# Forgetting attention: the key gates added inside VectorE's maxima, the output product on GpSimd, the roundings with a per-partition factor

## The reference

```
k, v = silu(conv4(x @ Wk)), silu(conv4(x @ Wv));  q = x @ Wq      # conv4: causal, 4 taps, per channel
q, k = rms_norm(q) * qnw, rms_norm(k) * knw                        # over the 64 channels of a head
c    = cumsum(log_sigmoid(x @ Wf + bf), over time)                 # one row per head
s    = q @ k.T / sqrt(64) + c[query] - c[key]                      # keys after the query are masked
o    = softmax(s) @ v
out  = (rms_norm(o) * onw * silu-like gate(x @ Wg)) @ Wo
```

## Time and profile before

| | |
|---|---|
| median of 3 runs | 2142.07 us (2141.72 to 2145.16) |
| the profiled execution | 2145.37 us, span 2143.5 us |
| the units of the stage in the trace | about 780 to 1735 us, the even part about 860 to 1640 us |
| busy over the whole span | TensorE 85%, VectorE 79%, ScalarE 66%, GpSimd 48% |

### The profile page before, as it was taken

The page is one execution under the profiler, slowest core; times in us unless marked ns, Lnnn a source line. Parts: engine busy times, 40 slices in busy tenths (PEclk is TensorE's granted clock), DMA queues, the critical chain, the costliest instruction groups (busy, mean ns, idle before and its releaser), DMA issues. The chain is left out here.

```text
span 2143.5 us, 36549 instructions
## 1 busy us (share of the span) xinstructions
PE 1823.9 (85%) x12003; PEld 880.1 (41%) x12003; DVE 1687.6 (79%) x2282; ACT 1409.8 (66%) x2322; POOL 1033.2 (48%) x1121
## 2 busy tenths in 40 slices
PE   5558886686978758999999999999999867789997
PEld 2113332553665413555555555555554423222222
DVE  5979997695349778888888888888887636698884
ACT  3547774574347646877777777777776524689994
POOL 0167774173106515666666776666666521431112
PEclk9869999798999989999999999999999978899999
DMA  3000000000000011112121121111111100422210
GB/s 97 0 15 0 0 0 0 1 0 1 0 0 1 1 58 52 53 63 60 51 62 62 63 62 58 62 56 59 63 63 62 36 16 20 99 79 56 59 47 40
DMA packets 71432, 84.49 MB, mean 39 GB/s; under 512 B 20544, under 2 KB 44032, under 8 KB 71168
## 3 DMA queue, kind: packets, MB, share of 16 engines
q1 hardware_dynamic: 69536, 81.69, 12.6%
q10 hardware_dynamic: 1728, 0.67, 0.1%
HBM read 71.95 MB, written 9.57 MB: 38 GB/s over the span
## 5 line engine op out<-in xcount | busy, mean ns | idle before, releaser
L1771 DVE SCALAR_TENSOR_TENSOR fu_kv<-fu_ps_kv,fa_vec,fu_kv 128x511 f32<-128x511 f32 (+2 forms) x384 | 285.7, 745 | 56.1 <-ACT fu_kv L1643 51.1
L1854 POOL TENSOR_TENSOR fu_ds<-fu_p 128x768 f32<-128x768 f32 x64 | 115.8, 1809 | 194.3 <-PE fu_ps_ss L1542 191.8
L2209 ACT ACTIVATE rt_p<-rt_ps_s 128x1024 f32<-128x1024 f32 x192 | 185.6, 1028 | 25.1 <-PE rt_ps_s L2140 25.1
L1502 PE MATMUL fu_ps_s<-fu_qn,fu_kn 64*128 64x512 f32 (+3 forms) x1024 | 190.0, 468 | 2.5 <-DVE fu_sg L1732 1.8
L625 POOL TENSOR_TENSOR scan_hC<-scan_h,scan_c 128x1024 f32<-128x1024 f32 x64 | 150.8, 2356 | 72.0 <-DVE scan_h L601 72.0
L1643 ACT ACTIVATE fu_kv<-fu_ps_kv,fa_vec 128x512 f32<-128x512 f32 x128 | 88.3, 690 | 111.0 <-PE fu_ps_kv L1551 66.6
L1532 PE MATMUL fu_ps_n<-fu_p,fu_vt 128*64 128x512 f32 (+3 forms) x1024 | 151.9, 439 | 0.0
L524 PE MATMUL scan_ps_y<-scan_hC,w_ident 128*128 128x512 f32 x256 | 125.7, 614 | 26.4 <-POOL scan_hC L625 14.9
L601 DVE TENSOR_TENSOR_SCAN scan_h<-scan_dA,scan_ps_b 128x1024 f32<-128x1024 f32 x64 | 146.4, 2287 | 2.2
L2105 POOL TENSOR_SCALAR rt_d<-rt_d 128x1024 f32<-128x1024 f32 x32 | 34.9, 1091 | 184.1 <-DVE rt_d L2230 178.4
L1870 POOL TENSOR_TENSOR fu_kn<-fu_ks,fu_rb 128x512 f32<-128x512 f32 x64 | 81.4, 1272 | 75.2 <-DMA fu_rb<-rms_rows 75.0
(11 more groups left out here) (384 smaller groups left out, 5291.4 us busy)
## 6 DMA issues: line engine op xcount, KB each, us to landing
fu_rb<-rms_rows SPq DMA_DIRECT2D x256, 128.0 KB, 2.9
fu_ro<-rms_rows SPq DMA_DIRECT2D x128, 128.0 KB, 3.0
ra_stackq<-rope_parts SPq DMA_DIRECT2D x168, 32.0 KB
ra_stackk<-rope_parts SPq DMA_DIRECT2D x168, 32.0 KB
w_X<-in_xT SPq DMA_DIRECT2D x4, 512.0 KB, 6.6
fa_wp<-in_wp SPq DMA_DIRECT2D x8, 256.0 KB
fa_cr<-ncum_rows SPq DMA_DIRECT2D x128, 3.0 KB
rope_parts<-ra_hi SPq DMA_DIRECT2D x16, 128.0 KB, 3.1
```

The source lines that it names most:

```text
L1502: pe.matmul(sps[:, h, at:at + T - t * P], k[head(h), t * P:(t + 1) * P], q[head(h), t * P:T], start=(at == 0), stop=False)
L1771: dve.scalar_tensor_tensor(acc, kvps[:, at, 0:T - j], vec[:, a % GA, w:w + 1], acc, ALU.mult, ALU.add).then_inc(done, 1)
L1854: pool.tensor_tensor(DS[:, :, :], P0[p % 2][:, :, P:T], P13[:, :, 0:3 * P], ALU.add).then_inc(s.d1, 1)
L2209: act.activation(p[:, :, :], sps[unit(g, t, i) % RING][:, :, :], ACT.Exp, scale=DH_B ** -0.5).then_inc(s.exp, 1)
```

## The change

Four edits. (1) The key gates are no longer added by TensorE: the 8 matmuls per unit with `w_pick` go. Instead `cum` is stored to DRAM in fp32 (`ncum`), two rows per unit are loaded with broadcast to 128 partitions (`fu_nb`, 512 KB, one DMA, behind the 4 loads of `fu_rb`), and VectorE adds them while it takes the maximum, by `tensor_tensor_reduce`, one instruction per head and block. (2) The output product `fu_og` moves from VectorE to GpSimd; its per-channel weight is folded into `fa_wo` once. (3) The roundings, which can no longer take a negated maximum, multiply by a per-partition -1 (`w.neg`) in `scalar_tensor_tensor`. (4) The loads of `fu_nb` wait until the maxima of the unit that held the buffer before are done.

```diff
 # forget_gates, SP
+                sp.wait_ge(s.cum, 1)
+                sp.dma_start(ncum_dram, cum[:, :]).then_inc(held.kept, 16)
 # forget_units, SP, behind the four loads of RB
+                        row = HEADS_A * n + 2 * g
+                        sp.wait_ge(s.red, seen(u - 1, 2 * NT))
+                        sp.dma_start(NB[u % 2][:, :, :], ncum_dram[row:row + 2, :].rearrange("(o h) t -> o h t", o=1).broadcast_to([P, 2, T])).then_inc(nbs[u % 2], 16)
 # TensorE
-                    for t, at in blocks:
-                        for h in range(2):
-                            pe.matmul(mps[:, h, at:at + (t + 1) * P], w.pick[head(h), :], cr[head(h), 0:(t + 1) * P], start=False, stop=False)
-                        pe.wait_ge(crs[m % 3], 32 * (m // 3 + 1))
 # VectorE
+                def greatest(u, t, at):
+
+                    cols = (t + 1) * P
+                    for h in range(2):
+                        sums = mps[:, h, at:at + cols]
+                        dve.tensor_tensor_reduce(sums, sums, NB[u % 2][:, h, 0:cols], 1.0, LOWEST, ALU.add, ALU.max, top[:, t, h:h + 1]).then_inc(s.red, 1)
-                        dve.tensor_reduce(nm[:, 1, :], mps[:, :, 0:2 * P], AX_X, ALU.max, negate=True).then_inc(s.red, 1)
+                        greatest(b, 1, 0)
-                        dve.tensor_copy(MHL[:, :, :, 3], nm[:, :, :]).then_inc(s.hi, 1)
+                        dve.scalar_tensor_tensor(MHL[:, :, :, 3], top[:, :, :], w.neg[:, 0:1], MHL[:, :, :, 0], ALU.mult, ALU.mult).then_inc(s.hi, 1)
-                        dve.tensor_tensor(MHL[:, :, :, 4], nm[:, :, :], MHL[:, :, :, 3], ALU.subtract).then_inc(s.ml, 1)
+                        dve.scalar_tensor_tensor(MHL[:, :, :, 4], top[:, :, :], w.neg[:, 0:1], MHL[:, :, :, 3], ALU.mult, ALU.subtract).then_inc(s.ml, 1)
-                    if real(o):
-                        output(o)
 # GpSimd, behind the gated numerator and ahead of the root's iterations
+                    if real(o):
+                        pool.wait_ge(s.gated, o + 1)
+                        pool.wait_ge(ros[o % 2], 32 * (o // 2 + 1))
+                        pool.wait_ge(s.wo, o // 2)
+                        pool.tensor_tensor(OG[o % 2][:, :], NUM[o % NR][:, :], RO[o % 2][:, :], ALU.mult).then_inc(s.og, 1)
```

More of the change, by code:

```diff
@@ L1249, in forgetting_attention_stages, with forget_gates @@
 def forgetting_attention_stages(nc, w, X, XN):
+    ncum_dram = nc.dram_tensor("ncum", (P, T), F32, kind="Internal").ap()
     ncum_rows = nc.dram_tensor("ncum_rows", (P, KF, T), BF16, kind="Internal").ap()
     with Stage(nc, "fa") as outer:
-        loaded, stored = outer.sems("loaded stored")
+        loaded, stored, kept = outer.sems("loaded stored kept")
         held = named(
             wp=outer.sb("wp", [P, GA, 4, P]), wo=outer.sb("wo", [P, GA, P]), vec=outer.sb("vec", [P, GA, 3 + 2 * TAPS]), nc=outer.sb("nc", [P, KF, T], BF16), cr=[outer.sb(f"cr{k}", [P, T], BF16) for k in range(3)], mhl=outer.sb("mhl", [P, NT, 2, DH_A], BF16),
-            loaded=loaded, stored=stored,
+            loaded=loaded, stored=stored, kept=kept,
         )
-        forget_gates(nc, w, XN, ncum_rows, held)
-        forget_units(nc, w, X, XN, ncum_rows, held)
-def forget_gates(nc, w, XN, ncum_rows, held):
+        forget_gates(nc, w, XN, ncum_dram, ncum_rows, held)
+        forget_units(nc, w, X, XN, ncum_dram, ncum_rows, held)
+def forget_gates(nc, w, XN, ncum_dram, ncum_rows, held):
     with Stage(nc, "fg") as st:
@@ L1328, in _, with forget_units @@
                 dve.tensor_copy(NC[:, 2, :], r2[:, :]).then_inc(s.lo, 1)
-def forget_units(nc, w, X, XN, ncum_rows, held):
+def forget_units(nc, w, X, XN, ncum_dram, ncum_rows, held):
     U = B * GA
@@ L1337, in forget_units @@
     KR, VR, NR = 7, 3, 6
+    LOWEST = -3.0e38
     THIRDS = ((0, slice(0, P)), (1, slice(P, 320)), (3, slice(320, T)))
@@ L1388, in forget_units @@
         RR = st.sb("rr", [P, T], BF16)
-        nm = st.sb("nm", [P, NT, 2])
+        top = st.sb("top", [P, NT, 2])
+        NB = [st.sb(f"nb{k}", [P, 2, T]) for k in range(2)]
         SG = st.sb("sg", [P, T])
@@ L1450, in _ @@
                 sp.wait_ge(held.stored, 16)
+                sp.wait_ge(held.kept, 16)
                 for i in range(-AHEAD, U + OUT + 2):
@@ L1568, in _ @@
                         g = o % GA
-                        pe.wait_ge(s.red, seen(b + 1, 4))
+                        pe.wait_ge(s.red, seen(b + 1, 2 * NT))
+                        pe.wait_ge(s.set, 5)
+                        pe.wait_ge(s.x, o // 2)
                         pe.wait_ge(s.og, o + 1)
@@ L1761, in _ @@
                 dve.wait_ge(held.loaded, 16 * (GA + 2))
+                dve.wait_ge(held.kept, 16)
                 for i in range(-AHEAD, U + 1):
@@ L1830, in _ @@
                 add(last - 3)
-                output(last - 2)
                 begin(U + 1)
                 gate(last + 1)
-                output(last - 1)
                 add(last - 1)
-                output(last)
-                output(last + 1)
                 add(last + 1)
@@ L1845, in _ @@
                 pool.tensor_scalar(qw[:, :], qw[:, :], 0.5 * DH_A ** -0.5, None, ALU.mult).then_inc(s.set, 1)
+                pool.memset(SG[:, :], 0.0).then_inc(s.set, 1)
                 pool.tensor_scalar(ow[:, :], vec[:, :, 2], 0.25, None, ALU.mult).then_inc(s.set, 1)
-                pool.memset(SG[:, :], 0.0).then_inc(s.set, 1)
-                for i in range(-AHEAD, U + OUT + 1):
-                    d, p, c, u = i + AHEAD - 1, i - 1, i - OUT, i + 2
+                pool.wait_ge(s.set, 4)
+                pool.tensor_tensor(wo[:, :, :], wo[:, :, :], ow[:, :].rearrange("p (g o) -> p g o", o=1).broadcast_to([P, GA, P]), ALU.mult).then_inc(s.set, 1)
+                for i in range(-AHEAD, U + OUT + 2):
+                    d, p, c, o, u = i + AHEAD - 1, i - 1, i - OUT, i - OUT - 1, i + 2
                     if real(p):
@@ L1874, in _ @@
                         pool.tensor_tensor(NUM[c % NR][:, :], NUM[c % NR][:, :], SG[:, :], ALU.mult).then_inc(s.gated, 1)
-                    q, o = windows(i - 2) if i % WIN == 0 else (None, None)
-                    if q is not None or o is not None:
-                        j, r = (i - 2) // WIN + 3, slice(0, rows_of(q, o).stop)
+                    if real(o):
[3 more added lines that the diff above has]
+                        pool.tensor_tensor(OG[o % 2][:, :], NUM[o % NR][:, :], RO[o % 2][:, :], ALU.mult).then_inc(s.og, 1)
+                    q, v = windows(i - 2) if i % WIN == 0 else (None, None)
+                    if q is not None or v is not None:
+                        j, r = (i - 2) // WIN + 3, slice(0, rows_of(q, v).stop)
                         if j < ENDING:
@@ L2302, in hybrid_kernel @@
         for name in EARLY + LATER:
-            tile(name, BF16 if name in ("pick", "eye2", "mask2", "past2", "identb") else F32)
+            tile(name, BF16 if name in ("eye2", "mask2", "past2", "identb") else F32)
         for name, shape in (("u0", [P, P]), ("vo0", [P, P]), ("bias1", [P, 1]), ("gate", [P, FF]), ("up", [P, FF]), ("down", [P, KF, P]),
```

30 lines of the change are left out of this document (12 added, 18 removed).

## The result

The changed kernel takes 2165.96 us in the median of 4 runs (2157.10 to 2169.12), beside 2143.61 for the kernel before in the same runs: a ratio of 1.0104 [1.0085, 1.0122], so 22 us slower. The forecast was 2131, faster. The profiled execution took 2162.96 us, with a span of 2160.9.

What follows compares the result with a forecast made beforehand. TensorE was taken as the bound, VectorE hardly behind. Each pair gains 0.44 us less 0.1 for the roundings, 0.34 times 32 = 11 us: 2134.4 for the profiled execution, so 2131 against 2142.07; 8-in-10 range 2113 to 2163.

Steps and rivals of the forecast that it cites:

- What bounds the kernel, and the pair: Even part of the stage: TensorE bounds, VectorE hardly behind; a pair of steps takes 27.4 us instead of 27.78.
- TensorE's saving, and the price of the new instructions: Per unit: TensorE saves 0.55 us without `w_pick`; VectorE's maxima cost 0.15 us fixed per half, +0.87 in all.
- Rival 1: VectorE's maxima cost the upper bound, 0.31 us per half; 21 us slower, 2163; chance 0.22.
- The roundings, "a loose end" of 0.1 us per pair: Short step: roundings slip ahead of GpSimd's third sum, 0.4 us earlier, or are held, 0.25 later; 0.1 us per pair lost.
- I see no reason why they should be freer.: VectorE's new roundings read two SBUF tiles, so GpSimd instructions hold them as they held the cast, 0.69 us.
- Which may push `fu_ro` by 3 us; then GpSimd waits inside the 5.63.: Long step: the `fu_nb` load ahead may delay `fu_ro` 3 us, within GpSimd's 5.63 us of idle time.
- Rival 5: Long step: `fu_og` on GpSimd holds VectorE's query by 0.6 us, 19 us in all; 2150; chance 0.08.
- 0.44 gained: The pair of steps closes 0.44 us early, before 0.1 us is taken off for the roundings.
- Rival 3: Short step: the new rounding is free of GpSimd, 0.20 us instead of 0.69; 27 us gained, 2115; chance 0.10.
- Rival 4: Edits cancel: fixed part near 0.2 us, rounding held in most steps (0.3 per pair); 2.6 us gained, 2139.5; chance 0.15.
- The DMA wait caps TensorE's lead: VectorE's bit operation, ahead of block 1's maximum, waits for `fu_var`'s DMA and is only 0.11 us early; TensorE's 0.4 is lost.
- The 14 us ahead of the roundings' term: Whole stage: 32 pairs, each 0.44 us shorter, gain 14 us before the roundings' 0.1 us per pair is subtracted.

Runs made afterwards that it cites:

- experiment 4: Changed kernel with roundings reading the maxima from PSUM (negating reduction, cast, subtraction: three instructions for two); 2127.98 us, 0.9916 of the kernel before.
- experiment 2: Kernel before with only `fu_og` moved from VectorE to GpSimd, old maxima and roundings; 2148.15 us, 1.0017 of the kernel before.
- experiment 1: Changed kernel with `fu_og` back on VectorE ahead of the query; 2159.44 us, 1.0076 of the kernel before.
- experiment 3: Changed kernel with the load of `fu_nb` issued behind the store of the roots and the loads of `fu_ro`; 2177.45 us, 1.0160 of the kernel before.
- experiment 9: Changed kernel with `fu_og` on GpSimd replaced by two memsets of its tile, which read nothing; 2175.78 us, 1.0159 of the kernel before.
- experiment 5: Changed kernel with roundings from PSUM and the `fu_nb` load behind the roots' store and `fu_ro` loads; 2116.37 us, 0.9873 of the kernel before.
- experiment 10: Experiment 5 with the root's bit operation moved behind the roundings of the next step; 2106.24 us, 0.9832 of the kernel before.
- experiment 7: Kernel before with only the roundings changed, to read the maxima from PSUM; 2134.49 us, 0.9961 of the kernel before.
- experiment 8: Kernel before with `fu_og` on GpSimd and roundings reading the maxima from PSUM; 2128.39 us, 0.9932 of the kernel before.
- experiment 6: Changed kernel with roundings from PSUM and `fu_og` back on VectorE; 2141.00 us, 1.0001 of the kernel before.

## Why the prediction was wrong

- **What bounds the kernel, and the pair.** Right for one half of the pairs: 13 took 27.35 to 27.71 us, where 27.4 was forecast. They are not free of holds; their roundings cost as much as in the pairs of 27.78 before (1.7 us, where those took 1.7 to 2.1). The stage got slower by the other half.
- **TensorE's saving, and the price of the new instructions.** The mechanism was right and the term too dear: about 0.1 us fixed per half, 0.15 taken. Rival 1, for which the pitch of 512 columns had to be above 0.75 us, is false, with a pitch of 0.60 and 0.65. That its 2163 lies near the measured 2166 is chance.
- **The roundings, "a loose end" of 0.1 us per pair.** This is the step that failed. The working put one hold against one place of the old schedule, the start of the short step, and let GpSimd move by 0.55 us with TensorE. At that place the roundings rose from 0.93 to 1.19 us. The larger part came at the start of the long step, which the working left out (1.04 us before, 1.56 after, from 0.5 to 3.5): there the sums do not wait for TensorE but follow the root, and the prediction itself had the root end 1.3 us later. Measured over all: 0.35 us per unit more than before, 0.7 per pair, where 0.1 was taken. A small part is the new form itself, which takes 0.26 and 0.25 us when free, against 0.18 and 0.20 of the old one. In experiment 4, where nothing holds them, the result changes its sign, by 38 us. The row that should have warned was already there: a cast of 8 columns at 0.69 us beside a remainder at 0.20 says that the chain behind it costs whatever GpSimd happens to do.
- **"I see no reason why they should be freer."** Right, but the second rounding became less free, which was not asked. Where the first is held by one partial sum, the second and the next sum start within 0.02 us of each other. The old remainder started within 0.005 us of the sum in 45 units and was held in none; in 6 it came 0.006 us or more behind, and was held. In experiment 2, with the old form, it was 52 free and none held. The new form came 0.006 to 0.016 us behind the sum in all 31 such units of the changed kernel, and in 43 to 51 each of experiments 1, 3 and 9, and was held every time. No run changes the form of the roundings alone, so what this costs in time stays open.
- **"Which may push `fu_ro` by 3 us; then GpSimd waits inside the 5.63."** The wait was there, but GpSimd had also come later, and `fu_og` ran beside the query. Idle ahead of `fu_og` is now 90 us in the 740 read, and ahead of the first sum 32, where 161 stood. Rival 5 had just this mechanism, with a chance of 0.08, since it asked for a landing within half a microsecond of one place. It needs no such luck: an instruction of 1.27 us and one of 0.74 overlap over a width of 2 us, 42 of 56 did, and 33 of them were held. It took 0.32 us per unit on VectorE, 0.64 per pair, where rival 5 had 0.6. But it seems to have cost little time here: the short pairs have the longer queries, and experiments 1, 3 and 9, with free queries, took 2159 to 2177 us.
- **The two together** add 1.3 us per pair on VectorE, against 0.44 gained. The pair became 0.6 longer and not 0.9. The roundings' 0.7 less the 0.44 gives 0.3 of the 0.6; what makes up the rest no run separates.
- **Rivals.** Rival 3 (a free rounding) described what experiment 4 then built, 2128 against its 2115, the query being held. Rival 4's reason, a held rounding, was right, and its 0.3 us per pair less than half of what came.
- **The DMA wait caps TensorE's lead.** Right: in experiment 5 it is 0.64 us, and moving it off the chain (experiment 10) gives 10 us.
- **The 14 us ahead of the roundings' term.** Not confirmed as it stands. With free roundings on both sides the edits as they were made gain 7 us (experiment 4 against 7; 9, each against its own kernel before), with the query held. With the gate load also behind the store, which is no part of the change, they gain 18 (5 against 7): the move of `fu_og` is 6 of them (8 against 7) and the gates in the maxima 12 (5 against 8), in this order. The other way round they don't add up so (experiment 6).

The Trainium skill (page "SBUF — State Buffer", section "SBUF: two separate sides") says that VectorE and GpSimd share a pair of ports, locked for a whole instruction: a VectorE instruction with two SBUF inputs fully blocks against a GpSimd one that reads SBUF. The runs agree: the query takes 0.74 us beside fills and up to 1.83 behind a product that started first, and the roundings with one input in PSUM take 0.19. The prediction named this rule and drew from it only that the new form was no better; what it did not ask is how often each such instruction meets one of GpSimd's.

Open is why the new form of the rounding comes a hundredth of a microsecond later than the old one, and why experiment 6 stands 7 us above experiment 7.

## What to carry to other kernels

Before work moves to GpSimd, list VectorE's instructions with two SBUF inputs on the critical chain (and copies within SBUF, as the cast here), the smallest first, at every place of the period: each can cost a whole GpSimd instruction, and a shift of either engine moves the collision and does not remove it. Remove it by the form (one operand in PSUM), and only then judge a change of order, whose sign may turn: the later gate load lost 11 us before that and gained 9 to 12 after. A period that varies from pair to pair, as 27.5 and 29.7 here, can be a sign of such meetings; sort the pairs by the time of the suspected instructions to see which of them pays. A steady period is no proof of the opposite: in experiment 3 nearly every pair had the same hold.

## What the runs showed of the hardware

- A maximum with an accumulator write shows as two instructions in the trace, but costs only about 0.1 us beyond its columns, since the write (0.14 us) overlaps the next one.
- The hold works both ways: in experiment 4 `fu_og` took 1.56 us where it takes 1.27, started 0.32 us behind a query. Between 0.04 and 0.33 us behind a query it took 1.56 to 1.84 us in all five cases, and the query 0.74 or 0.75.

```profile
1238.27 0.74 DVE L1826 SCALAR_TENSOR_TENSOR fu_qn<-fu_qs,fu_qw,fu_rb 128x512 f32<-128x512 f32 x1
```

```profile
1238.59 1.56 POOL L1889 TENSOR_TENSOR fu_og<-fu_num,fu_ro 128x512 f32<-128x512 f32 x1 [0.88 <-POOL fu_num L1884]
```

- A reduction that reads 8 columns in SBUF and writes PSUM was never held (0.170 us in mean in 53 cases), while a cast of as many columns within SBUF was, with one SBUF input: 0.18 us free, 1.26 at most in the kernel before, 2.03 in experiment 2.
